# A graph layer by sorted one-hots: sixteen-bit pair comparisons for the key and slot one-hots, spills handled two quads at a time, and a quad streamed in two chunks of ten and seven ranges

## What is computed

```python
h = jnp.maximum(_layernorm(x, axis=-1), 0.0)          # x: 6250 x 64
h_src = feat[src]                                     # 200000 edges, dst sorted
for r in range(16):
    mask = etypes == r
    msg = msg + h_src * mask[:, None] @ weight[r]     # weight[r]: 64 x 64
out = jax.ops.segment_sum(msg, dst, num_segments=6250)
return x + out
```

## Time and profile before

| | |
|---|---|
| median of 3 runs | 1113.21 us (1111.95 to 1114.58) |
| the profiled execution | 1110.19 us, its span 1108.4 us |
| PE busy | 958.2 us (86%) |
| DVE busy | 910.3 us (82%), 3137 instructions |
| POOL busy | 807.5 us (73%), 644 instructions |
| ACT busy | 530.7 us (48%) |
| mean granted PE clock | 0.966 |

### The profile page before, as it was taken

The page is one execution under the profiler, slowest core; times in us unless marked ns, Lnnn a source line. Parts: engine busy times, 40 slices in busy tenths (PEclk is TensorE's granted clock), DMA queues, the critical chain, the costliest instruction groups (busy, mean ns, idle before and its releaser), DMA issues.

```text
span 1108.4 us, 57958 instructions
## 1 busy us (share of the span) xinstructions
PE 958.2 (86%) x24205; PEld 809.6 (73%) x24205; DVE 910.3 (82%) x3137; ACT 530.7 (48%) x1548; POOL 807.5 (73%) x644
## 2 busy tenths in 40 slices
PE   3999988899988888988899888989799798888996
PEld 1445777788877777877788777778687687776885
DVE  7755889898888689887899887998788689886884
ACT  4886454454445345544444453544344345444441
POOL 3231888888888888888787887878888888887760
PEclk9998999999999899998999998999999999998998
DMA  6697322222322222222232222232222222221312
GB/s 183 259 391 287 81 69 63 64 64 75 82 65 66 63 64 65 64 66 64 67 85 66 65 63 66 63 85 67 64 66 64 64 65 65 68 82 45 87 44 61
DMA packets 42713, 98.10 MB, mean 89 GB/s; under 512 B 14749, under 2 KB 14751, under 8 KB 42452
## 3 DMA queue, kind: packets, MB, share of 16 engines
q1 hardware_dynamic: 14870, 45.60, 12.3%
q0 software_dynamic: 19616, 20.13, 10.7%
q10 hardware_dynamic: 7966, 28.64, 6.7%
HBM read 66.69 MB, written 27.62 MB: 85 GB/s over the span
## 4 chain that ended last, share of the span: by engine, by line
PE 42%; DVE 26%; issue 12%; ACT 7%; POOL 7%; DMA 5%; DVEq 2%; ACTq 1%; POOLq 0%
PE ps L1288 15%; PE ps L1305 13%; DVE u L964 9%; POOL u L532 6%; DVE u L954 4%; PE ps L1329 4%; ACT u L605 3%; DMA u<-table,row_idx 3%; PE ps L1343 3%; DVE spreadv L872 2%; DVE accT L980 2%; ACT u L691 2%; DMA table<-u 2%; DVE rank L834 2%; PE ps L1210 1%
## 5 line engine op out<-in xcount | busy, mean ns | idle before, releaser
L532 POOL DMA_INDIRECT u<-table,row_idx x575 | 740.8, 1288 | 210.7 <-issue 140.5
L674 ACT CAST u<-ps 128x384 bf16<-128x384 f32 (+1 forms) x684 | 294.5, 465 | 443.5 <-PE ps L1288 433.3
L1288 PE MATMUL ps<-parts,u 128*128 128x192 bf16 x3724 | 356.2, 250 | 0.7 <-ACT key_p L595 0.5
L1288 PEld LDWEIGHTS ps<-parts,u 128*128 128x128 bf16 x3724 | 308.8, 99 | 11.5 <-issue 7.8
L1305 PE MATMUL ps<-u 32*64 32x272 bf16 (+1 forms) x15808 | 297.2, 279 | 8.4 <-issue 8.2
L964 DVE TENSOR_SCALAR u<-iota_key,z_sb 128x272 bf16<-128x272 f16 x1292 | 280.9, 286 | 8.8 <-DVE win_x L862 6.9
L1305 PEld LDWEIGHTS ps<-u 32*64 32x64 bf16 x15808 | 227.4, 105 | 49.7 <-issue 31.8
L954 DVE TENSOR_SCALAR u<-u,node_id 128x1152 bf16<-128x1152 f16 (+1 forms) x456 | 197.0, 487 | 0.0
L691 ACT COPY u<-ps 128x272 f32<-128x272 f32 (+3 forms) x304 | 102.0, 421 | 60.8 <-PE ps L1305 60.8
L980 DVE TENSOR_TENSOR accT<-accT,u 128x17 f32 (+1 forms) x392 | 71.3, 182 | 65.0 <-DVE accT L980 26.2
L1329 PE MATMUL ps<-u,w_cat 128*64 128x136 f32 x1216 | 90.4, 289 | 6.7 <-issue 5.2
(11 more groups left out here) (134 smaller groups left out, 769.9 us busy)
## 6 DMA issues: line engine op xcount, KB each, us to landing
u<-rel_dram SPq DMA_DIRECT2D x76, 544.0 KB
table<-u ACTq DMA_DIRECT2D x24, 1024.0 KB, 5.2
u<-table,row_idx POOLq DMA_INDIRECT x575
rel_dram<-rel_row SPq DMA_DIRECT2D x76, 4.2 KB
x_sb<-x SPq DMA_DIRECT2D x2, 448.0 KB
out<-h_sb SPq DMA_DIRECT2D x3, 224.0 KB
out<-h_sb ACTq DMA_DIRECT2D x3, 224.0 KB
msg_x<-table,spill_row POOLq DMA_INDIRECT x38
```

The source lines that it names most:

```text
L532: pool.indirect_dma_start(out=msg_p[:, b, j, :], out_offset=None, in_=table, in_offset=bass.IndirectOffsetOnAxis(ap=row_idx[:, j, m:m + 1] ...
L674: act.copy(msg_s[:, u % MB, 0:width, :].rearrange("p q c -> p (q c)"), ps[gather_bank(u)][:, 0:width * ROW]).then_inc(s_gev, 1)
L1288: last = pe.matmul(there, hot[:, part % HRING, t - q * SK, at * P:(at + 1) * P], parts[:, t, :], start=t == blocks[0], stop=t == blocks[-1])
```

## The change

Seven edits, most of them on DVE.

1. `key_hots` makes all ranges of a chunk in one `tensor_tensor` of two 16-bit inputs, 10 x 272 and 7 x 272 elements, in place of 17 `tensor_scalar` of 272. So that the second input has neighbouring elements, ACT writes every value of `z_sb` twice, as 16-bit pairs. `placed` uses the same pair form (`rank2`, `spill_rank`), with one more small copy.
2. `source_hots` makes a whole quad's one-hot in three instructions of 2176, 2048 and 2048 elements in place of six of 1152 to 896; there are two whole buffers in place of three halves.
3. Spills are masked every quad, but ranked, placed and permuted once for two quads.
4. A quad is streamed in two chunks (ranges 0 to 9 and 10 to 16) in place of three.
5. The adds become a generator, and DVE issues one after each of its larger instructions in place of all in a row.
6. The sorting works on 128 partitions in place of 104; POOL fills the new rows with -1 and makes two more constants at the start.
7. The order of some steps on PE and ACT and the estimates of `spots` move accordingly.

```diff
-    CHUNKS = ((0, 3), (3, 6), (6, GB))
+    CHUNKS = ((0, 5), (5, GB))
...
+            pool.memset(vals[96:P, :, :, :], -1.0).then_inc(s_const, 1)
...
                 for a in range(WINS):
                     rows = slice(a * CAP, (a + 1) * CAP)
-                    act.copy(z_sb[rows, g % 3, :, :].rearrange("p v q -> p (v q)"),
-                             ps[6][rows, a * 2 * SQ:(a + 1) * 2 * SQ]).then_inc(s_zev, 1)
+                    seen = ps[6][rows, a * 2 * SQ:(a + 1) * 2 * SQ].rearrange("p (c o) -> p c o", o=1).to_broadcast([CAP, 2 * SQ, 2])
+                    act.copy(z_sb[rows, g % 3, 0:4 * SQ].rearrange("p (c o) -> p c o", o=2), seen).then_inc(s_zev, 1)
...
+            def placed(hots, first, ranks, tiles, n):
+
+                there = hots.rearrange("p t (h o) -> p t h o", o=2)
+                places = iota_slot[:, first:first + n].rearrange("p (t h o) -> p t h o", t=1, o=2).to_broadcast([P, tiles, n // 2, 2])
+                mine = ranks.rearrange("p t (h o) -> p t h o", h=1).to_broadcast([P, tiles, n // 2, 2])
                 return dve.tensor_tensor(there, places, mine, ALU.is_equal)
...
-            def key_hots(n, low, high):
+            def source_hots(n, k):
+                there = min(SQ, (NT - k + SK - 1) // SK)
+                if k == 0:
+                    dve.wait_ge(s_bc[n % BCR], 16 * (n // BCR + 1))
+                    if n >= HRING:
+                        dve.wait_ge(s_gat, GB * (n - HRING + 1))
+                last = dve.tensor_scalar(hot[:, n % HRING, k, 0:there * P], bc[:, n % BCR, 0:there * P], node_id[:, k:k + 1], None,
+                                         ALU.is_equal)
+                if k == SK - 1:
+                    last.then_inc(s_hot, 1)
+
+            def key_hots(n, c):
+                own, part = ranges_of(n, c), n * len(CHUNKS) + c
                 dve.wait_ge(s_zev, WINS * (n + 1))
-                for q in range(low, high):
-                    v = n * SQ + q
-                    if v >= KR:
-                        dve.wait_ge(s_agg, v - KR + 1)
-                    dve.tensor_scalar(khot[:, v % KR, :], iota_key[:, :], z_sb[:, n % 3, 1, q:q + 1], None, ALU.is_equal).then_inc(s_khot, 1)
+                if part >= KR:
+                    dve.wait_ge(s_agg, (n - KR // len(CHUNKS)) * SQ + own[-1] + 1)
+                there = khot[:, part % KR, 0:len(own), :].rearrange("p q (h o) -> p q h o", o=2)
+                keys = iota_key[:, :].rearrange("p (q h o) -> p q h o", q=1, o=2).to_broadcast([P, len(own), KEYS // 2, 2])
+                mine = z_sb[:, n % 3, 2 * (SQ + own[0]):2 * (SQ + own[-1] + 1)].rearrange("p (q h o) -> p q h o", h=1, o=2)
+                dve.tensor_tensor(there, keys, mine.to_broadcast([P, len(own), KEYS // 2, 2]), ALU.is_equal).then_inc(s_khot, 1)
...
             for n in range(NPR):
                 ahead, sorting = n + 1 < NPR, n + 2 < NPR
+                adds = add_sums(n - 2) if n >= 2 else iter(())
                 if sorting:
                     sort_slots(n + 2)
                     sort_values(n + 2)
+                    next(adds, None)
                     if n + 3 < NPR:
                         sort_ranges(n + 3)
+                        next(adds, None)
                 if ahead:
-                    source_hots(n + 1, 0)
-                if n >= 2:
-                    add_sums(n - 2)
+                    for k in range(SK):
+                        source_hots(n + 1, k)
+                        next(adds, None)
+                    key_hots(n + 1, 0)
+                    next(adds, None)
+                if n % 2 == 0:
+                    spilled_rows(n // 2)
                 if ahead:
-                    key_hots(n + 1, KEYS_AT[0], KEYS_AT[1])
-                if sorting:
-                    sort_spilled(n + 2)
-                if ahead:
-                    source_hots(n + 1, 1)
+                    key_hots(n + 1, 1)
+                    next(adds, None)
                 for m in sums_in[n + 1] if ahead else ():
                     gathered_hots(m)
-                if ahead:
-                    key_hots(n + 1, KEYS_AT[1], KEYS_AT[2])
...
+                    next(adds, None)
+                for _ in adds:
+                    pass
```

More of the change, by code:

```diff
@@ L154, in gnn_program @@
                     spots.append(now)
-        now += 0.38 * (turned(n, c) is not None) + 0.31 * (spilled(n, c) is not None)
+        now += 0.22 * (permuted(n, c) is not None) + 0.12 * (turned(n, c) is not None) + 0.25 * (spill_ranked(n, c) is not None)
         if i:
@@ L162, in gnn_program @@
                 now += 0.125 if 2 * b + 1 < SQ else 0.063
-        now += 0.5 * (c == 1 and n > 0) + 0.22 * (permuted(n, c) is not None) + 0.45 * (ranked(n, c) is not None)
+        now += 0.5 * (c == 1 and n > 0) + 0.25 * (spill_placed(n, c) is not None) + 0.25 * (ranked(n, c) is not None)
         if n >= 2 and n % 2 == 0 and c == weigh_at:
@@ L691, in take_sums @@
                     act.copy(agg[:, n % 2 * WINS + a, 0:width], ps[AGG[a]][:, 0:width]).then_inc(s_aev, 1)
-            for n, c in STREAM:
+            for i, (n, c) in enumerate(STREAM):
                 take_messages(n, c)
-                if turned(n, c):
-                    take_rel(turned(n, c))
-                if spilled(n, c) and spilled(n, c) % 2 == 1:
-                    take_spilled(spilled(n, c))
-                if c == 2 and n in TURNS_AT:
-                    take_last(TURNS_AT.index(n))
+                if spill_placed(n, c) is not None:
+                    take_spilled(spill_placed(n, c))
                 if c == 0 and n >= 1:
@@ L704, in _ @@
                     take_z(permuted(n, c))
+                if turned(n, c):
+                    take_rel(turned(n, c))
+                if c == 1 and n in TURNS_AT:
+                    take_last(TURNS_AT.index(n))
             take_sums(NPR - 1)
@@ L998, in add_weighed @@
                     for i, base in enumerate(bases_of(2 * GR * g + first, GR)):
-                        add(slice(0, P), base, SW, of[:, (first + i) * SW:(first + i + 1) * SW])
+                        yield from add(slice(0, P), base, SW, of[:, (first + i) * SW:(first + i + 1) * SW])
             def add_sums(n):
@@ L1012, in add_sums @@
                         rows = slice(0 if len(tiles_of(m)) > 1 else tiles_of(m)[0] % 2 * D, P)
-                        add(rows, base, PW, agg[rows, n % 2 * WINS + 1, sum_place(m)])
+                        yield from add(rows, base, PW, agg[rows, n % 2 * WINS + 1, sum_place(m)])
             dve.wait_ge(s_turn_s, 6)
@@ L1226, in sort_turn @@
                 pe.wait_ge(s_zev, WINS * (g + 1))
-                pe.transpose(ps[6][0:SQ, 0:P], z_sb[:, g % 3, 0, :], ident[:, :]).then_inc(s_relT, 1)
+                pe.matmul(ps[6][:, 0:P], z_sb[:, g % 3, 0:2 * P:2], ident16[:, :], start=True, stop=True).then_inc(s_relT, 1)
             piece(0)
@@ L1287, in gather @@
                     for t in blocks:
-                        last = pe.matmul(there, hot[:, part % HRING, t - q * SK, at * P:(at + 1) * P], parts[:, t, :],
+                        last = pe.matmul(there, hot[:, n % HRING, t - q * SK, q * P:(q + 1) * P], parts[:, t, :],
                                          start=t == blocks[0], stop=t == blocks[-1])
@@ L1305, in sums @@
                         last = pe.matmul(ps[AGG[a]][half * D:(half + 1) * D, keys], msg_s[rows, u % MB, q % 2, part * D:(part + 1) * D],
-                                         khot[rows, v % KR, keys], start=q == 0 and part < 2, stop=(q, part) == (SQ - 1, 2))
+                                         khot[rows, chunk % KR, q - ranges_of(n, c)[0], keys], start=q == 0 and part < 2, stop=(q, part) == (SQ - 1, 2))
                     return last
+                pe.wait_ge(s_khot, chunk + 1)
                 for b in banks_of(n, c):
```

256 lines of the change are left out of this document (129 added, 127 removed).

## The result

The changed kernel takes 1045.9 us (median of 4 runs, 1040.6 to 1046.4) against 1112.6 us before (4 runs beside it): a ratio of 0.939, 95% interval 0.936 to 0.943. The forecast was 1206 us, slower; the time lies in its range of 1027 to 1300, and near rival A (1027). The sign was wrong.

A forecast was written before the change was run, and what follows sets the result against it. POOL's fetches were taken to bound the loop; 3.85 us lost a quad plus 0.05, against 2.68, gave +1.22 us times 76, +93 us: 1203 on the profiled execution, 1206 us as median, range 1027 to 1300.

The forecast's parts named there:

- rival A: Pair key comparisons do not hold POOL's fetches off; only ranges and source comparisons count: -86 us, 1027 us, chance 0.24.
- POOL bounds the kernel before: In the loop, POOL's 612 fetches set the length, 12.77 us a quad, as POOL waits for nobody.
- PE and DVE alone, 12.15 us a quad: The loop's pace by PE and DVE without POOL, from one permutation to the next: 13.01 and 11.29 us, mean 12.15.
- A fetch reads 0.13 us in, is held, and needs 0.82 us more: POOL's fetch reads about 0.13 us after its start, cannot while DVE holds it off, then needs 0.82 us more.
- Source 2.14 us, keys 1.55 and 1.13: DVE's new comparisons a quad: three source ones 2.14 us (2.57 before), two key ones 2.68 together (3.70 before).
- the walk: POOL's fetches followed through DVE's turns: 4.7 us lost with one addition, 3.0 with eight; mean 3.85 against 2.68, +93 us.
- Worth nothing while POOL bounds, 1.4 us a quad if not: Spill and slot one-hots, spill matmuls and permutation lead on DVE and PE: no gain under POOL, otherwise some 1.4 us a quad.
- At the start nothing: Before the loop, about 6 us of new POOL filling hides in 7.95 us of POOL's idle time: no cost.
- Signs: Profile features expected after the change, such as mean fetch 1.43 us, single fetches of 4 us and more, permutation wait gone.

## Why the prediction was wrong

**POOL bounds the kernel before** was right. Without the fetches it is 60 us faster, and 61 us less of fetches (additions spread) made it 53 us faster. PE and DVE alone, 12.15 us a quad, came to 47 us below the loop; the run without fetches says 60 in all and 12.11 a quad from its first gather to its last (920.4 / 76).

**A fetch reads 0.13 us in, is held, and needs 0.82 us more** was right, and so was that the new pair comparisons hold it: 561.69 + 0.82 = 562.51. Rival A, whose time was nearest, had the wrong mechanism and came near by luck: it had 1.55 us lost a quad and nothing beside the key comparisons, and of the 1.33 measured more than half, 57 of 101 us, belongs to fetches whose read falls in one of them. The Trainium skill, "SBUF — State Buffer", section "Who interferes with whom", infers that an instruction with two SBUF inputs leaves descriptor making alone; this row, the fetch of 501.49 that is held through two key comparisons, and the 66 us that short key comparisons give back to the fetches disagree with it.

**Source 2.14 us, keys 1.55 and 1.13** were right: 2.12, 1.56 and 1.18.

**The step that failed is the walk**: "the fetch that wants its read at 1.25 gets it at 6.6", one fetch in a turn with one addition, four in 8.0 us in one with eight. It gave 3.85 us lost a quad; measured are 101 / 76 = 1.33, against 2.68 before. Two things in it were wrong. The first is the rule: that adjacent long instructions let no fetch in until the chain ends. It came from two fetches, at 574.76 and 581.02, which were passed over. In the changed kernel the fetch of 560.66 got in between two adjacent key comparisons, and of the reads that fall well inside a source comparison with another close behind it 32 of 32 got in at the end of the one they fell in. The second is that I let every fetch be caught at the start of the chain. A fetch whose read falls shortly before a comparison ends loses 0.1 to 0.3 us, and the next starts 0.3 us after it ends, so that the moments of a whole turn hang on each other. In the changed kernel 121 reads fall in the source comparisons, and they lose 21 us together; before, 111 reads fall there and lose 131 of the 203 us. (A read is taken as 0.13 us behind the fetch's start, from 110 us on, over the whole trace.)

What stays open is the condition under which a held fetch gets in at a boundary. Length of the instructions, a small instruction between them, and an addition between them each fail as a rule in one of the runs above. The moment of the read fails too. These are all reads that fall 0.14 to 0.16 us into the first source comparison of a turn, where the instruction ahead of it runs straight into it:

| kernel | ahead of it | reads | held | lost by one, us |
|---|---|---|---|---|
| before | ranges | 51 | 51 | 1.25 to 2.12 |
| before, one small instruction a quad | ranges | 49 | 49 | 1.25 to 2.12 |
| before, sources joined | ranges | 31 | 31 | 1.99 to 2.07 |
| before, additions spread | ranges | 10 | 10 | 2.11 to 2.12 |
| before, additions spread | an addition | 36 | 0 | 0.0 |
| changed, additions in a row | ranges | 15 | 0 | 0.0 |

(Split sources and short keys in the changed kernel would add 4 and 3 reads to the last row, none of them held.) The fourth and fifth rows say that an addition ahead of the chain did free these fetches in the kernel before; the last says that the changed kernel frees them without. One of its fetches and DVE beside it:

```profile
540.61 0.94 POOL L540 DMA_INDIRECT msg_x<-table,spill_row  x1 [0.30 <-PE ps L1313]
```

```profile
540.23 0.44 DVE L839 TENSOR_TENSOR ranges<-vals,iota_range 128x272 f16<-128x272 f16 x1
540.59 2.13 DVE L977 TENSOR_SCALAR u<-u,node_id 128x2176 bf16<-128x2176 f16 x3
```

The joined kernel has source comparisons of the same sizes and holds all 31 through them. Its ranges run on 104 partitions and these on 128 (the sixth edit), but no run changes that alone, and in the changed kernel itself the fetches of 560.66 and 585.24 came out differently at the same place of the chain. Such a term can't be forecast from two places; its sign was open, and I gave slower 0.71.

**Worth nothing while POOL bounds, 1.4 us a quad if not** was too large and had no wait set against it. The loop without fetches is 0.63 us a quad shorter. The prediction did not price the two chunks at all: five banks in a row on three PSUM banks make PE wait 1 us a quad for ACT (0.84 in the run without fetches, 64.2 us). With three chunks the changed kernel is some 23 us faster (1112.6 x (0.939 - 0.918)), and POOL's window fell by 23.

**At the start nothing** missed 8 us. POOL's filling was hidden from POOL, but not from DVE. The changed kernel, POOL and then DVE:

```profile
4.39 5.16 POOL L498 MEMSET vals<- 32x6080 f16 x1
```

```profile
6.59 3.41 DVE L787 TENSOR_SCALAR u<-u 128x832 f32<-128x832 int32 x1 [6.59 <-DMA u<-src]
10.03 3.75 DVE L788 TENSOR_SCALAR u<-u 128x832 f32<-128x832 f32 x1
```

and DVE in the kernel before:

```profile
6.82 0.59 DVE L767 TENSOR_SCALAR u<-u 128x832 f32<-128x832 int32 x1 [6.82 <-DMA u<-src]
7.44 0.59 DVE L768 TENSOR_SCALAR u<-u 128x832 f32<-128x832 f32 x1
```

Two one-input instructions take 7.2 us in place of 1.2, and they end with POOL's fillings: the first 0.45 us after this one (9.55), and the second lies beside two more. These 6 us would be most of the 8 by which the first fetch is late; no run moves the filling. I had looked at what hides the filling on POOL and not at whom the filling holds up.

**Signs.** Of those named, POOL without a pause over 0.31 us, the mean fetch of 1.43 us (681.8 / 613 = 1.11), single fetches of 4 us (3.18 at most) and PE's waits for fetches failed; the durations at 990, DVE's busy share (down by over a tenth, from 82% to 74%) and the permutation's wait held. POOL waits for its signs now, which the prediction had named as a sign against it.

## What to carry to other kernels

When an engine that never pauses bounds the kernel and another engine holds it off, the loss depends on where its instructions fall in the other's chain; count it over all of them from the trace, and treat an edit to the order of that chain as able to move it: the same spreading of additions took 61 us off in one kernel and nothing in the other, with no work changed. A new grouping of work needs its own look at the ring it goes round: five banks in a row on three is a wait in every round. And a filling moved to an idle engine must be looked at from the engine that it may hold up, here DVE, not only from its own idle time.

## What was not expected of the hardware

- A pair instruction of DVE (two 16-bit inputs, innermost dimension of two) takes 1561 ns for 2720 elements and 1176 for 1904, and holds off an indirect fetch of POOL whose read falls well inside it, at least until it ends; short one-input comparisons of 272 columns in its place let the mean fetch fall from 1.104 to 1.001 us.
- A held fetch may get in at the first boundary of two DVE instructions (1.85 us), or pass two (3.17) or three (4.00), where an undisturbed one takes 0.94. Of reads 0.14 to 0.16 us into the source comparison of 2176 columns, straight behind the ranges, 31 of 31 are held in one kernel and 0 of 15 in another.
- A filling of 32 x 6080 elements on POOL (5.16 us) made one-input DVE instructions of 832 columns take 3.41 and 3.75 us in place of 0.59.
- In two rounds of runs the 15808 short matmuls of 32 rows were slower, idle for 156 us and busy for 441 in place of 5 and 296, and the kernel before took 1378 us in place of 1105 to 1113; one of the two chip numbers stands for a round of 1105 us as well.
